# Row maxima of the second attention: short diagonal pieces of several heads in one PSUM bank

## The reference, cut to what matters

```
q, k, v = h @ wq, h @ wk, h @ wv        # 16 query heads, 4 key/value heads, head size 64
q, k = rope(q), rope(k)                 # each key head serves 4 query heads
scores = q @ k.T / 8 + causal_bias      # (1024 x 1024) for each batch entry and query head
x = clip(x + softmax(scores) @ v @ wo, -100, 100)
x = clip(x + moe(rms(x)), -100, 100)    # top 2 of 8 experts
```

## Time and profile before

| | |
|---|---|
| median of 3 runs | 3838.05 us |
| the profiled execution | 3821.54 us, span 3819.2 us |
| TensorE matmuls (PE) | 3384.5 us busy, 89% of the span |
| VectorE (DVE) | 2759.9 us, 72% |
| GpSimd (POOL) | 2031.2 us, 53% |
| ScalarE (ACT) | 1672.0 us, 44% |
| chain that ended last | PE 66%, DVE 14%, issue 9%, POOL 6% |
| L1166, maxima scores | 1536 matmuls, 399 ns mean |
| L1169, masks of them | 1024 matmuls, 237 ns mean |
| L1501, reductions | 1024 + 512 instructions, 583 and 483 ns mean |

### The profile page before, as it was taken

One profiled execution on the slowest core, in us unless ns is written; L12 is line 12 of the kernel. 1 busy time (PEld: TensorE's weight loads), 2 busy tenths in 40 slices (PEclk: granted clock), 3 DMA queues, 4 the chain that ended last, 5 costly groups with the idle time before them and its releaser, 6 DMA issues.

```text
span 3819.2 us, 65097 instructions
## 1 busy us (share of the span) xinstructions
PE 3384.5 (89%) x18456; PEld 2247.9 (59%) x18456; DVE 2759.9 (72%) x4711; ACT 1672.0 (44%) x3133; POOL 2031.2 (53%) x1615
## 2 busy tenths in 40 slices
PE   5899999739999979699999795999998869999897
PEld 2455555426666657466666574666656646666575
DVE  7877787358788756588886566887856668888566
ACT  3266666423444345334443453344334524444344
POOL 2100000036878646368787463778774638787654
PEclk9589899959999989799999897999998979999999
DMA  0000000043324101333331013333310134232001
GB/s 15 1 1 2 2 1 1 17 104 75 85 68 91 28 6 39 76 74 81 76 76 26 9 36 80 84 67 84 70 24 13 37 83 92 61 90 68 9 17 30
DMA packets 113175, 181.33 MB, mean 47 GB/s; under 512 B 26560, under 2 KB 54080, under 8 KB 112576
## 3 DMA queue, kind: packets, MB, share of 16 engines
q1 hardware_dynamic: 112832, 177.26, 20.1%
HBM read 23.45 MB, written 2.10 MB: 7 GB/s over the span
## 4 chain that ended last, share of the span: by engine, by line
PE 66%; DVE 14%; issue 9%; POOL 6%; ACT 3%; DMA 1%; SPq 1%; POOLq 0%; DVEq 0%; ACTq 0%
PE psO L1196 11%; PE psA L1184 7%; PE psA L1166 6%; PE psA L1185 6%; DVE rden L1459 4%; PE psO L1052 3%; PE psA L1040 3%; PE psA L1029 3%; PE psA L1272 3%; POOL xw L764 3%; PE psA L1274 3%; PE psA L1273 3%; PE psO L1215 2%; PE psO L1208 2%; PE psA L1169 1%
## 5 line engine op out<-in xcount | busy, mean ns | idle before, releaser
L905 ACT ACTIVATE prob<-psA 128x512 f32<-128x512 f32 x1152 | 658.4, 597 | 1083.7 <-PE psA L1185 321.9
L764 POOL TENSOR_TENSOR xw<-xw,prob 128x512 f32<-128x512 f32 x672 | 882.4, 1313 | 180.1 <-ACT prob L905 100.0
L1501 DVE TENSOR_REDUCE mxp<-psA 128x1 f32<-128x512 f32 (+3 forms) x1024 | 542.5, 583 | 129.4 <-PE psA L1166 118.8
L1184 PE MATMUL psA<-qs,ks 128*128 128x512 f32 x1152 | 539.0, 468 | 26.3 <-DMA qs<-mrow 21.9
L1459 DVE RECIPROCAL rden<-psO 128x256 f32<-128x256 f32 x256 | 449.2, 1755 | 153.5 <-PE psO L1208 116.9
L1166 PE MATMUL psA<-ks,qs 128*128 128x512 f32 (+3 forms) x1536 | 496.2, 399 | 50.7 <-DMA qs<-normed 49.0
L788 POOL TENSOR_TENSOR hidl<-hid,hidh 128x512 fp32r<-128x512 f32 x256 | 330.8, 1298 | 284.7 <-ACT hidh L943 284.5
L764 POOL TENSOR_TENSOR xw<-prob 128x512 f32<-128x512 f32 x224 | 291.7, 1302 | 353.3 <-ACT prob L905 265.7
L1185 PE MATMUL psA<-qs,ks 128*128 128x512 f32 x1152 | 455.4, 395 | 0.0
L1166 PEld LDWEIGHTS psA<-ks,qs 128*128 128x128 f32 x1536 | 299.9, 202 | 101.9 <-issue 53.7
L1400 DVE TENSOR_REDUCE mxp<-psA 128x1 f32<-128x512 f32 x512 | 315.2, 682 | 40.4 <-PE psA L1029 40.4
(11 more groups left out here) (244 smaller groups left out, 6454.3 us busy)
## 6 DMA issues: line engine op xcount, KB each, us to landing
qs<-normed SPq DMA_DIRECT2D x384, 256.0 KB, 4.9
rbp<-rb SPq DMA_DIRECT2D x256, 192.0 KB, 3.5
est<-in_L_ffn_wg SPq DMA_DIRECT2D x32, 128.0 KB, 2.1
est<-in_L_ffn_wu SPq DMA_DIRECT2D x32, 128.0 KB, 2.1
est<-in_L_ffn_wd SPq DMA_DIRECT2D x64, 64.0 KB, 1.9
wst<-in_L_ffn_wq SPq DMA_DIRECT2D x4, 512.0 KB, 4.4
wos<-in_L_ffn_wo SPq DMA_DIRECT2D x64, 32.0 KB, 2.1
outer_kept<-outer SPq DMA_DIRECT2D x1, 1024.0 KB, 6.4
```

The source lines that it names most:

```text
L764: g.tensor_tensor(psum_k[:, t % 2, :], before, prob[:, i % 4, :], ALU.add).then_inc(s_su, 1 if kt > 1 else 2 + (t == 1))
L905: act(prob[:, k % 4, :], psS[:, k % 2, :], ACT.Exp, scale=float(HD) ** -0.5).then_inc(s_ex, 1)
L1184: mm(psS[:, i % 2, :], ks[b][:, 0, tile], qs1[b][:, c, :, qs], start=True, stop=False)
L1501: vec.tensor_reduce(dst, ring[SLOT["M", n, t, m] % N_RING][:, 0:k1 - k0], AX.X, ALU.max).then_inc(s_mr, 1)
```

## The change

`max_pieces` now walks over key ranges first and puts w heads side by side in one bank where their piece is short: w = max(1, 512 // (keys - k0)). Pieces of 128 columns become one of 4 heads (512 columns), pieces of 256 become two of 2 heads; the others stay. A piece is then w matmuls, one mask matmul whose moving operand repeats the 128 mask columns w times and whose output is the last 128 columns of each head's stretch, and one reduction that gives w maxima. The order of the pieces in the ring changes with it, since key ranges are now outside and heads inside. The plan's costs for M are other ones. s_rw becomes one semaphore for each half, and the two places that wait for it count by head.

```diff
 def max_pieces(t):
     keys = (t + 1) * P
-    return [(h, k0, min(k0 + CH, keys)) for h in range(GQ) for k0 in range(0, keys, CH)]
+    return [(h, w, k0, min(k0 + CH, keys)) for k0 in range(0, keys, CH) for w in (max(1, CH // (keys - k0)),)
+            for h in range(0, GQ, w)]
...
-            stage("tensor", item, max(200, (k1 - k0) / 2.3) + 100 * (k1 == (t + 1) * P), ("land", ("Q", n, t // TPC)),
+            stage("tensor", item, w * max(115, (k1 - k0) / 2.2) + (90 + w * 35) * (k1 == (t + 1) * P), ("land", ("Q", n, t // TPC)),
...
-            then("vector", item, 80 + 1.04 * (k1 - k0), ...)
+            then("vector", item, 150 + 1.04 * w * (k1 - k0), ...)
...
+        s_rw = [sem(f"max2_in_stack_{c}") for c in range(NCH)]
...
-                                     mrow2[c][:, :].bitcast(F32)).then_inc(s_rw, 16)
+                                     mrow2[c][:, :].bitcast(F32)).then_inc(s_rw[c], 16)
...
-                            a.wait_ge(s_rw, 16 * (u - 1))
+                            a.wait_ge(s_rw[c], 16 * it)
...
-                    ins = mm(bank[:, 0:k1 - k0], qs1[b][:, c, h, t % TPC * P:(t % TPC + 1) * P], ks[b][:, 0, k0:k1],
-                             start=True, stop=not diagonal)
+                    for i in range(w):
+                        ins = mm(bank[:, i, :], qs1[b][:, c, h + i, t % TPC * P:(t % TPC + 1) * P], ks[b][:, 0, k0:k1],
+                                 start=(i == 0), stop=not diagonal)
                     if diagonal:
-                        ins = mm(bank[:, k1 - k0 - P:k1 - k0], identb[:, :], maskq[:, :], start=False, stop=True)
+                        ins = mm(bank[:, :, k1 - k0 - P:k1 - k0], identb[:, :], maskq[:, :].unsqueeze(1).broadcast_to([P, w, P]),
+                                 start=False, stop=True)
...
-                        t_.wait_ge(s_rw, 16 * (it * NCH + c + 1))
+                        t_.wait_ge(s_rw[c], 16 * (it + 1))
...
-                        vec.tensor_reduce(dst, ring[SLOT["M", n, t, m] % N_RING][:, 0:k1 - k0], AX.X, ALU.max).then_inc(s_mr, 1)
+                        vec.tensor_reduce(dst, bank, AX.X, ALU.max).then_inc(s_mr, 1)
```

More of the change, by code:

```diff
@@ L232, in attention_order @@
             t, m = part
-            _, k0, k1 = max_pieces(t)[m]
-            stage("tensor", item, max(200, (k1 - k0) / 2.3) + 100 * (k1 == (t + 1) * P), ("land", ("Q", n, t // TPC)),
+            _, w, k0, k1 = max_pieces(t)[m]
+            stage("tensor", item, w * max(115, (k1 - k0) / 2.2) + (90 + w * 35) * (k1 == (t + 1) * P), ("land", ("Q", n, t // TPC)),
                   ("vector", ("K", n, t // TPC)), *turn)
-            then("vector", item, 80 + 1.04 * (k1 - k0), ("tensor", item), ("tensor", ("J", n - 1, t // TPC)) if n else None)
+            then("vector", item, 150 + 1.04 * w * (k1 - k0), ("tensor", item), ("tensor", ("J", n - 1, t // TPC)) if n else None)
         else:
@@ L475, in program @@
         s_ad, s_hi, s_lo, s_kl, s_dup = sem("roped"), sem("stack2_high"), sem("q_stack2_low"), sem("k_stack2_low"), sem("stacks2_stored")
-        s_ms, s_mr, s_jt, s_mc, s_rw = (sem("max2_scores"), sem("max2_taken"), sem("max2_turned"), sem("max2_copied"),
-                                        sem("max2_in_stack"))
+        s_ms, s_mr, s_jt, s_mc = (sem("max2_scores"), sem("max2_taken"), sem("max2_turned"), sem("max2_copied"))
+        s_rw = [sem(f"max2_in_stack_{c}") for c in range(NCH)]
         s_qk, s_ex, s_su, s_pv = sem("scores2"), sem("exp2"), sem("probabilities_summed"), sem("pv2")
@@ L1163, in maximum @@
                     bank = bank_of(("M", n, t, m))
-                    h, k0, k1 = max_pieces(t)[m]
+                    h, w, k0, k1 = max_pieces(t)[m]
+                    bank = bank[:, 0:w * (k1 - k0)].rearrange("p (h n) -> p h n", h=w)
                     diagonal = k1 == (t + 1) * P
-                    ins = mm(bank[:, 0:k1 - k0], qs1[b][:, c, h, t % TPC * P:(t % TPC + 1) * P], ks[b][:, 0, k0:k1],
-                             start=True, stop=not diagonal)
+                    for i in range(w):
+                        ins = mm(bank[:, i, :], qs1[b][:, c, h + i, t % TPC * P:(t % TPC + 1) * P], ks[b][:, 0, k0:k1],
+                                 start=(i == 0), stop=not diagonal)
                     if diagonal:
-                        ins = mm(bank[:, k1 - k0 - P:k1 - k0], identb[:, :], maskq[:, :], start=False, stop=True)
+                        ins = mm(bank[:, :, k1 - k0 - P:k1 - k0], identb[:, :], maskq[:, :].unsqueeze(1).broadcast_to([P, w, P]),
+                                 start=False, stop=True)
                     ins.then_inc(s_ms, 1)
@@ L1491, in _ @@
                         t, m = i
-                        c, (h, k0, k1) = t // TPC, max_pieces(t)[m]
+                        c, (h, w, k0, k1) = t // TPC, max_pieces(t)[m]
                         if m == 0 and t % TPC == 0:
@@ L1498, in _ @@
                         v.wait_ge(s_ms, it * N_MAX2 + PIECES[t] + m + 1)
-                        col = h * TPC + t % TPC
-                        dst = mxp[:, k0 // CH, col:col + 1] if c else mxq[:, 0, col:col + 1]
-                        vec.tensor_reduce(dst, ring[SLOT["M", n, t, m] % N_RING][:, 0:k1 - k0], AX.X, ALU.max).then_inc(s_mr, 1)
+                        dst = (mxp[:, k0 // CH, :] if c else mxq[:, 0, :]).rearrange("p (h t) -> p h t", t=TPC)[:, h:h + w, t % TPC]
+                        bank = ring[SLOT["M", n, t, m] % N_RING][:, 0:w * (k1 - k0)].rearrange("p (h n) -> p h n", h=w)
+                        vec.tensor_reduce(dst, bank, AX.X, ALU.max).then_inc(s_mr, 1)
                     elif what == "X":
```

## The result

The changed kernel takes 3883.79 us (median of 4 runs, 3878.39 to 3886.20) beside 3835.94 us for the kernel before: a ratio of 1.0128, 95% interval 1.0113 to 1.0143. It is 48 us slower; 3814 was predicted.

The account below looks back on a forecast made before the run. The prediction took TensorE, 98% busy in the attention stretch, as the limit; 21.6 us from cheaper pieces plus 3.0 from head 0's reductions made 24.6, rounded to 24: 3838 - 24 = 3814 us, range 3798 to 3832.

Parts of the forecast that it names:

- So the TensorE queue is the limit of this stretch.: Attention from 1660 to 2071 us: TensorE 98% busy, so time taken off the maxima's matmuls should shorten it.
- rival A: TensorE's saved time is given back as waiting between engines: 3833 us, a gain of 0 to 7; chance 0.14.
- The prices of the pieces: Maxima on TensorE: 0.63 us per four-wide piece, 0.39 per two-wide; 0.77 saved a head, 21.6 us in all.
- VectorE and head 0: Lighter reductions count only in head 0's second half: 0.75 us a layer, 3.0 us for four layers.
- The semaphores: Row waits of ScalarE and TensorE: both end when they did, no wait is added, 0.
- The plan: New order on all queues: priced at zero; one couple of turns in each of 28 heads is 10 us either way.
- C: Coarser pieces make the plan turn more often; 2.4 more couples a head cancel the gain, 3.5 give 3849; chance 0.10.
- B: The two-wide mask's strided output runs at half rate, losing 12 us: 3826 us; chance 0.09.
- D: The order gets better, with less idle time and fewer turns, 10 to 15 us more gain: 3801 us; chance 0.12.
- If the turns are 24 or more: Test named as showing the forecast wrong: turns of direction per head in the stretch, 20 before.
- a busy share below 97%: Test named as showing the forecast wrong: TensorE's busy share in the stretch, 98% before.

Follow-up runs that it names:

- e11: Kernel before in its own order, with the 1024 mask matmuls of the maxima left out: 3808 us, ratio 0.9945.
- e12: Wide pieces in the order of the kernel before, each where the first of its narrow pieces stood: 3832 us, ratio 0.9994.
- e1: Wide pieces and row semaphores in the order of the kernel before, each where the last of its narrow pieces stood: 3849 us, ratio 1.0039.
- e2: Changed kernel's order and banks, but each head's own 128-column mask and reduction as before: 3892 us, ratio 1.0163.
- e10: Order of e8, but inside each wide piece the masks and reductions of the kernel before: 3815 us, ratio 0.9944.
- e8: Changed kernel's instructions in another order, from the best of 432 sets of plan prices by the replay: 3800 us, ratio 0.9911.
- e3: Kernel before with one row semaphore for each half and nothing else: 3836 us, ratio 1.0009.
- e7: Changed kernel with the plan's price of a maxima piece on TensorE times 1.1, same instructions: 3856 us, ratio 1.0046.
- e5: Kernel before, narrow pieces and old prices, with key ranges outside and heads inside, plus the two row semaphores: 3894 us, ratio 1.0171.
- e9: Kernel before, narrow pieces, with the changed kernel's plan prices and the two row semaphores: 3835 us, ratio 1.0006.
- e1m: As e1, but each wide piece gets 2 or 4 separate 128-column masks instead of one broad mask: 3849 us, ratio 1.0035.

## Why the prediction was wrong

- **"So the TensorE queue is the limit of this stretch."** This step failed. 98% busy was read as: time taken off comes off the end. The runs show that in the old order 28% of it comes off for the masks (e11), nothing measurable for the wide pieces at the first place (e12, 0.9982 to 1.0006), and less than nothing at the last (e1). Two things stood behind the 98%. The rows' durations (0.39 us) are longer than the distances (0.235), so a wait of up to 0.16 us between two matmuls doesn't show as idle. And the maxima are filler: the plan had put them into gaps that TensorE had anyway, waiting for ScalarE's exponentials and VectorE's normalisations. In a run of maxima the next limit is VectorE, whose reductions free the banks (the second place in e11); rival A had named VectorE as the next limit, and left it out because it gets lighter. A filled gap looks like a busy engine.
- **The prices of the pieces.** Right: 0.63 us for a four-wide piece, 0.36 for 0.39, no cost of the strided mask, 691 ns for four outputs. In the order that shows no idle time they are worth about 15 of the 21.6 us counted, the lighter reductions included.
- **VectorE and head 0.** The last turned maxima of head 0 do come 1.1 us earlier, where 0.75 was counted, but not for the reason given. With the old masks and reductions in the new order they come as early (87.9 us after L1448 in e2 and 87.8 in the changed kernel, means of four layers), and with the wide pieces in the old order as late as before (89.0 in e1, 88.9 before). The order moved them; the lighter reductions gave at most 0.2 us (e10 against e8).
- **The semaphores.** Right: 0 (e3).
- **The plan "priced at zero, since neither sign is shown", with 10 us either way for a couple of turns.** This is the term that decided. Across the orders that I ran, attention goes from 559.0 to 578.3 us with identical instructions (e8, e7, changed), 77 us in the four layers, more than three times the sum that I worked out. The range came from the turns alone, when the order also sets idle time and how much attention work is left when the maxima run out.
- **Rivals.** C had the right sign and nearly its count: 24 turns for 20, two couples, against the 2.4 named as the point where the gain is gone. That is 0.7 us a head, less than the 0.89 that the pieces save, so C by itself would not have made the kernel slower. A holds too, as 1.4 us more idle time in each head. No rival had the end of the attention, 19.6 us longer for a middle 7.4 us shorter. B is out. D exists (e8), but it was found by a search over 432 plans and not by the change.
- **"If the turns are 24 or more"** was named as what would prove the forecast wrong, and did. So was a busy share below 97%: from 1680 to 2090 us it is 395.1 of 410 us, 96.4%.

What stays open: of the replay's six forecasts of a whole attention, four came out with the right sign and roughly the size (in us against before: e5 +12 for +17.6, e8 -12.6 for -7.7, e11 -7.4 for -8.0, e12 -0.8 for -1.8). It was too hopeful for e9 (-5 for -0.9) and had the sign wrong for e7 (-7 for +5.8). Applied afterwards to runs already measured it gave +8 for +11.6 (changed) and +4 for +3.1 (e1). Which wait it leaves out was not looked for, nor which wait makes e1 slower than e12.

## What to carry to other kernels

Where a fixed order is computed by a greedy plan, a change of piece sizes can be first of all another draw of the order; test the pieces in the old order, and several orders of the new pieces, before judging either. A busy share near 100% doesn't make an engine the limit if low-priority work was placed to fill it: take a known amount of that filler out and see how much comes off. A gain in the middle that leaves more behind is none: look at what remains when the filler runs out.

## What the runs showed that was not expected

Four full-width 128-column matmuls with weights of their own take (1846.47 - 1845.88) = 0.59 us, of which 0.18 belong to the mask before them. The rest is 0.07 for the first and 0.114 from the start of each of the other three to the next start. The Trainium skill ("TensorE: Matmul & The Clock Gate", section Back-to-back issue gap) gives 81 ns for a stream of such loads and matmuls; this case measures 114, and its measurement decides.

The part before the second attention is the same program in all these kernels, and yet in the profiled executions L1448 first starts at 797.6 us (e5), 798.6 (before), 811.0 (changed) or 816.8 (e1m). The 12 us between before and changed are most of why their profiled executions differ by 64 us and the medians by 48. That is the reason why attention times are given beside each run.
